# PE's order in a windowed attention: the products of probabilities by values of pair n-1 come ahead of the matmuls that add the maxima to the scores of pair n, not behind them

## The chip, the cores and the metric

The kernel runs on one core of a Trainium2 chip, in one launch. The metric is the device time of an execution in microseconds (us); lower is better.

## What is computed

The input x is 8 x 32 x 32 x 256 in float32. Two layers follow one another, each on a group-normalised copy of its input, each added back to it:

```python
x = x + _L0_conv_ref(_gn(x), qkv_w, qkv_b, bias_table)     # attention in windows of 8 x 8
x = x + _L1_conv_ref(_gn(x), W, b)                          # linear, then a spiking neuron over the 8 samples
# _L0_conv_ref, for each of 128 windows of 64 tokens and each of 16 heads of 16 channels:
attn = einsum('wihd,wjhd->whij', q * SCALE, k) + bias + MASK
attn = softmax(attn, axis=-1)
out  = einsum('whij,wjhd->wihd', attn, v)
```

_gn takes mean and variance of each sample in 32 groups of channels.

## The kernel before

x stays in SBUF for the whole run. The attention works on **strips**: a strip is one row of four windows (the code's `row`; 4 in a sample, 32 in all). A strip is worked off as two **pairs** of windows (n = 0 to 63). The code's k runs from 0 to 7 through the pairs of a sample; p = k % 2 is 0 for the first pair of a strip ("even pair") and 1 for the second ("odd pair"). The loop over samples 1 to 5 is a hardware loop, the others are written out.

Matmuls need more precision than one 16-bit or 32-bit reduced pass gives, so operands come as a high and a low part (xn_hi and xn_lo, k_hi and k_lo, v_hi and v_lo, p_hi and p_lo).

Every engine has its own program, in an order fixed by hand, and semaphores between them. In pair n:

- PE (TensorE): even pair: `project_q` and `project_k` of the next strip; odd pair: `project_v` of the next strip. Then `scores(n)`: bias and key-query products of the first half of the heads (L975, L977), the transpose of the maxima, `turn_maxima` (L992), the same products for the second half, and last the eight matmuls that add the negated maxima to the scores (L985). These eight wait until ScalarE has copied the transposed maxima (`max_rows`). They are called the **pick** matmuls here, after their weights, pick_max. Then `weigh_values(n-1)`: 24 matmuls of probabilities by values (L1008), here called **PV**, which in two pairs of a sample have a small matmul for the group statistics ahead of them (`beside`: L878 or L882). Then `max_scores(n+1)` (L952, L958), whose maxima will be needed by pair n+1, and `turn_attention(n-2)` (L1018).
- ACT (ScalarE): `normalise` or `xn_high` (even pair L461, odd pair L473, for the strip two ahead), `q_high` and `k_high` (L479, L492) or the first half of `v_high` (L501); `max_rows` (L570); in odd pairs the second half of `v_high`; then the four exponentials of pair n (L579, L580, two for each half of the heads), which wait for the pick matmuls; then `keep_attention(n-2)` (attn_cm, L543), which waits for `turn_attention`. In the trace's order of time, attn_cm and xn_hi or xn follow the exponentials.
- DVE (VectorE): low parts of q and k (L727, L739) or of v (L752); `attention_out(n-1)` (L769, L773), which waits for PV; the maxima of pair n+1 (neg_max, L759); statistics (L649).
- POOL (GpSimd): in odd pairs xn_lo (L386); p_lo of pair n (L424, after the exponentials); `add_attention(n-2)` (L413, after attn_cm); and once in a sample, in pair k = 2, 13 small instructions for the square roots of the next normalisation (L231 to L239). In the last sample they come at k = 4.
- SP: q and k of the next strip go to DRAM and come back stacked in another layout (k_spill, k_stack); `scores` of an even pair waits for them.

proj_ps holds q, k and v in turn: `project_q` waits until DVE has read the values (v_lo), and until xn_lo is there.

The first normalisation's set-up and the attention's first pairs share ACT, DVE and POOL with the building of bias tables (`bias_high`, `bias_variant`, `bias_low`). After the last pair come the LIF units (the spiking neuron), bound to each other in time order over the samples.

Of the kernel before, what the change touches and what calls it, by code (L numbers as in the profile page):

```python
# [5 lines left out]
def swin_attention_then_lif_kernel(nc, image, x, qkv_w, qkv_b, bias_table, lif_w, lif_b, out):  # L6
# [40 lines left out]
    with ctx:  # L47
# [134 lines left out]
        def wait(eng, s, value):  # L182

            if not isinstance(value, int) or value > 0:
                eng.wait_ge(s, value)
# [16 lines left out]
        def slot_total(row, y, per):  # L202

            return (row + (2 - y % 2)) * (per // 2)
# [5 lines left out]
        def is_first(n, lag):  # L210

            return isinstance(n, int) and n < lag

        def norm_beside(s, k):

            if has_sample(s, 1):
                return s + 1, (s + 1) * HALVES, HALVES, k - 1  # L220
            return SAMPLES, 0, EARLY, k - 3
# [19 lines left out]
        def is_last_pair(n):  # L241

            return isinstance(n, int) and n == PAIRS - 1

        def is_last_row(row, ahead=1):
            return isinstance(row, int) and row + ahead >= ROWS
# [626 lines left out]
        def _(pe):  # L873
            pe.wait_ge(const_step, 4)

            def average_means(norm, width, averages):
                pe.wait_ge(norm_dve, norm * NORM_STEPS + 1)
                pe.matmul(averages[:, 0:width], group_avg[:, :], moments[:, 0:width, 0], start=True, stop=True).then_inc(norm_pe, 1)  # L878

            def average_variances(norm, width, averages):  # L880
                pe.wait_ge(norm_dve, norm * NORM_STEPS + 4)
                pe.matmul(averages[:, NORMS:NORMS + width], group_avg[:, :], tiny[2][:, 0:width], start=True, stop=True)\  # L882
                  .then_inc(norm_pe, 1)
# [39 lines left out]
            def project_q(slot, r):  # L923
                pe.wait_ge(xn_lo_done, r + 1)
                wait(pe, v_lo_done, r)
                project_channels(banks[6], 0, xn_hi[slot], xn_lo[slot]).then_inc(q_ps_done, 1)

            def project_k(slot, r):
                wait(pe, attn_kept, 2 * r - 4)
                project_channels(banks[7], C, xn_hi[slot], xn_lo[slot], C).then_inc(k_ps_done, 1)  # L930

            def project_v(slot, r):
                pe.wait_ge(q_lo_done, r + 1)
                for p in range(2):
                    last = project_tokens(proj_ps[:, 0, p * C:(p + 1) * C], p, 2 * C, slot)
                last.then_inc(v_ps_done, 1)

            def variant(k, w):

                return 2 * (k // 2 == WROWS - 1) + (2 * (k % 2) + w == WCOLS - 1)  # L940
# [20 lines left out]
                                             start=False, stop=(h == 1 and mid == 1))  # L961
                last.then_inc(max_ps_done, 1)

            def scores(n, row, k):

                slot, p = k // 2 % 2, k % 2
                if p == 0:
                    pe.wait_ge(stacked[slot], slot_total(row, k // 2, 96))
                for h in range(HALVES):
                    wait(pe, p_hi_done, n * 2 + (h - 1))  # L970
                    for g in range(QUADS):
                        for w in range(2):
                            dst = score_ps[:, h, g * 128 + w * WS:g * 128 + (w + 1) * WS]
                            at = h * WCOLS + 2 * p + w
                            pe.matmul(dst, bias_k[:, variant(k, w), h * QUADS + g, :], both_parts[:, 0, :],  # L975
                                      start=(g == 0 and w == 0), stop=False)
                            pe.matmul(dst, k_stack[slot][:, g, at, :], q_stack[slot][:, g, at, :], start=False, stop=False)  # L977
                    if h == 0:
                        turn_maxima(n)
                pe.wait_ge(max_rows_done, n + 1)  # L980
                for h in range(HALVES):
                    for w in range(2):
                        for mid in range(2):
                            dst = score_ps[:, h, :].rearrange("p (m q w i) -> p m w q i", m=2, q=2, w=2)[:, mid, w, :, :]
                            last = pe.matmul(dst, pick_max[:, 4 * w + 2 * h + mid, :],  # L985
                                             max_rows[p][:, :].rearrange("p (q i) -> p q i", q=2),
                                             start=False, stop=(w == 1 and mid == 1))
                    last.then_inc(score_ps_done, 1)

            def turn_maxima(n):  # L990
                pe.wait_ge(neg_max_done, n + 1)
                pe.transpose(max_ps[:, 0, :].bitcast(f16)[0:16, 0:128], neg_max[:, :], ident_h[:, :])\  # L992
                  .then_inc(max_turned, 1)

            def weigh_values(m, row, k, beside=None):

                p = k % 2
                pe.wait_ge(p_lo_done, m * 2 + 2)
                if p == 0:
                    pe.wait_ge(v_lo_done, row + 1)  # L1000
                wait(pe, attn_done, m)
                if beside:
                    beside()
                for h in range(HALVES):
                    cols = pv_ps[:, h, 0:2 * WIN_N].rearrange("p (w g n) -> p w g n", w=2, g=QUADS)
                    for g in range(QUADS):
                        for at, (pp, vv) in enumerate(((p_hi, v_hi), (p_hi, v_lo), (p_lo, v_hi))):
                            last = pe.matmul(cols[:, :, g, :], pp[p][:, h * QUADS + g, :, :].rearrange("p w i -> p (w i)"),  # L1008
                                             vv[k][:, h, :, g, :, :].rearrange("p w e d -> p w (e d)"),
                                             start=(at == 0), stop=(at == 2))  # L1010
                last.then_inc(pv_ps_done, 1)

            def turn_attention(m, p):
                pe.wait_ge(attn_done, m + 1)
                wait(pe, attn_kept, m)
                tokens = attn[p][:, :, :, :].rearrange("p h n d -> p (h n d)")
                for h in range(HALVES):
                    last = pe.transpose(proj_ps[:, 1, h * 128:(h + 1) * 128], tokens[:, h * 128:(h + 1) * 128], ident[:, :])  # L1018
                last.then_inc(attn_turned, 1)
# [9 lines left out]
            def unit_products(m, t):  # L1029

                pe.wait_ge(unit_ready, m + 1)
                project_unit(banks[t], unit[t % 4]).then_inc(h_ps_done, 1)

            def pair(n, row, k, s):
                p = k % 2
                nxt = (k // 2 + 1) % 2
                if not is_last_row(row):
                    if p == 0:
                        project_q(nxt, row + 1)
                        project_k(nxt, row + 1)  # L1040
                    else:
                        project_v(nxt, row + 1)
                if is_first(n, 8):
                    pe.wait_ge(bias_lo_done, variant(k, 1) + 1)
                scores(n, row, k)
                norm, _, width, stage = norm_beside(s, k)
                beside = None
                if stage == 0:
                    beside = lambda: average_means(norm, width, spare_averages)
                if stage == 1:  # L1050
                    beside = lambda: average_variances(norm, width, spare_averages)
                if not is_first(n, 1):
                    weigh_values(n - 1, row if p else row - 1, (k - 1) % 4, beside)
                if not is_last_pair(n):
                    max_scores(n + 1, row + 1 if p else row, (k + 1) % BODY)
                if p == 0 and not is_last_row(row):
                    pe.wait_ge(k_lo_done, row + 2)
                if not is_first(n, 2):
                    turn_attention(n - 2, p)
                if is_last_pair(n):  # L1060
                    unit_products(0, 0)

            run(pe, pair)
            weigh_values(PAIRS - 1, ROWS - 1, 3)
            turn_attention(PAIRS - 2, 0)
# [50 lines left out]
```

## Time and profile before

| | |
|---|---|
| time of 3 runs | median 555.68 us (555.5 to 556.34) |
| the profiled execution | 557.95 us, its span 556.2 us |
| busy of the span: PE, weight loads | 475.5 us (85%), 425.9 us (77%) |
| busy: DVE, ACT, POOL | 445.3 us (80%), 415.5 us (75%), 272.0 us (49%) |
| granted TensorE clock, mean | 0.964 |

The attention takes most of the span: the first max_rows starts at 42.0 us and the last at 478.3 us. Before it is set-up, and after it are the LIF units. A timeline row of the trace gives the start in us, the duration, engine, line and operation; several equal instructions in a row are merged (xcount), and in square brackets stands how long the engine was idle before it and for what.

### The profile page before, as it was taken

Reading aid. Unit: us, or ns where it says so; the run is one execution under the profiler, and the core shown is the slowest. Engines: PE = TensorE matmul, PEld = TensorE weight load, DVE = VectorE, ACT = ScalarE, POOL = GpSimd, SP = SyncE. Lnnn points to the kernel's source line nnn. Section 1 sums busy time; section 2 is a strip of 40 time slices with the busy share of each in tenths; the row PEclk is TensorE's granted clock in tenths of the full one; section 3 lists DMA queues with packets and bytes.
Section 4 is the critical chain, followed back from the end, with each engine's and each line's share of the span. In section 5 each row is a group of like instructions: output and inputs, shape, how many; then the busy total and the mean of one; then the engine's idle time right before and its main releaser. Section 6 shows DMA issues by size and latency. Waiting matters only on the chain.

```text
span 556.2 us, 17802 instructions
## 1 busy us (share of the span) xinstructions
PE 475.5 (85%) x6504; PEld 425.9 (77%) x6504; DVE 445.3 (80%) x994; ACT 415.5 (75%) x1013; POOL 272.0 (49%) x379
## 2 busy tenths in 40 slices
PE   0364699898999899989998998999899977889997
PEld 0364688787888788888887887888788866778885
DVE  7856568868888889888987898788787877568897
ACT  2286578787889788888988998888889856745551
POOL 6134365556555656565566566655655546520000
PEclk9987789999999999999999999999999989879999
DMA  7176066766766677767776776656666545013333
GB/s 209 56 180 161 18 167 172 180 163 170 176 173 173 169 183 200 193 163 187 188 190 165 184 187 179 170 153 164 154 156 155 160 129 152 3 70 129 140 134 134
DMA packets 92576, 86.08 MB, mean 155 GB/s; under 512 B 41842, under 2 KB 63604, under 8 KB 92532
## 3 DMA queue, kind: packets, MB, share of 16 engines
q1 hardware_dynamic: 91808, 85.49, 58.0%
q8 instruction: 27, 0.44, 0.3%
q10 hardware_dynamic: 724, 0.01, 0.1%
q14 instruction: 17, 0.14, 0.1%
HBM read 47.72 MB, written 33.55 MB: 146 GB/s over the span
## 4 chain that ended last, share of the span: by engine, by line
PE 27%; issue 23%; POOL 22%; ACT 8%; DMA 8%; DVE 5%; SPq 3%; POOLq 1%; ACTq 1%; DVEq 0%
POOL p_lo L424 11%; POOL xc L413 5%; POOL xn_lo L386 4%; PE score_ps L895 3%; PE proj_ps L895 2%; PE pv_ps L895 2%; PE pv_ps L1008 2%; DMA k_stack<-k_spill1lo 2%; DMA k_spill1lo<-k_lo 2%; ACT v_hi L501 2%; PE proj_ps L908 2%; SPq L308 2%; PE max_ps L895 2%; PE score_ps L985 2%; PE proj_ps L910 2%
## 5 line engine op out<-in xcount | busy, mean ns | idle before, releaser
L424 POOL TENSOR_TENSOR p_lo<-probs,p_hi 128x512 f16<-128x512 f32 x128 | 146.6, 1166 | 165.0 <-ACT p_hi L580 165.0
L752 DVE TENSOR_TENSOR v_lo<-proj_ps,v_hi 64x128 f16<-64x128 f32 x256 | 74.1, 289 | 23.4 <-ACT v_hi L501 20.7
L579 ACT ACTIVATE probs<-score_ps 128x512 f32<-128x512 f32 x128 | 76.9, 601 | 19.5 <-PE score_ps L985 18.7
L975 PE MATMUL score_ps<-both_parts,bias_k 128*128 128x64 f16 x1024 | 83.1, 194 | 6.9 <-DMA k_stack<-k_spill1lo 4.0
L908 PE MATMUL proj_ps<-xn_hi,w_hi 128*128 128x256 f32 x256 | 76.7, 300 | 14.0 <-POOL xn_lo L386 13.4
L977 PE MATMUL score_ps<-q_stack,k_stack 96*128 96x64 f16 x1024 | 82.3, 194 | 0.0
L759 DVE TENSOR_REDUCE neg_max<-max_ps 128x16 f16<-128x1024 f32 x64 | 78.4, 1225 | 4.4 <-PE max_ps L958 2.4
L975 PEld LDWEIGHTS score_ps<-both_parts,bias_k 128*128 128x128 f16 x1024 | 67.7, 98 | 15.3 <-issue 4.6
L501 ACT ACTIVATE v_hi<-proj_ps 64x128 f16<-64x128 f32 x256 | 71.6, 280 | 10.1 <-PE proj_ps L920 7.1
L580 ACT ACTIVATE p_hi<-score_ps 128x512 f16<-128x512 f32 x128 | 77.3, 604 | 0.0
L909 PE MATMUL proj_ps<-xn_lo,w_hi 128*128 128x256 f32 x256 | 73.5, 287 | 0.0
L910 PE MATMUL proj_ps<-xn_hi,w_lo 128*128 128x256 f32 x256 | 73.3, 286 | 0.0
L977 PEld LDWEIGHTS score_ps<-q_stack,k_stack 96*128 96x128 f16 x1024 | 69.8, 98 | 0.0
L908 PEld LDWEIGHTS proj_ps<-xn_hi,w_hi 128*128 128x128 f32 x256 | 50.1, 196 | 19.3 <-issue 9.0
L739 DVE SCALAR_TENSOR_TENSOR k_lo<-proj_ps,parity_mask,k_hi 128x512 f16<-128x512 f32 x64 | 45.1, 746 | 21.6 <-ACT k_hi L492 21.6
L985 PE MATMUL score_ps<-max_rows,pick_max 128*128 128x128 f16 x512 | 41.2, 226 | 19.8 <-ACT max_rows L570 19.5
L1008 PE MATMUL pv_ps<-v_hi,p_hi 128*128 128x68 f16 x512 | 57.0, 198 | 0.5 <-POOL p_lo L424 0.5
L1008 PE MATMUL pv_ps<-v_lo,p_hi 128*128 128x68 f16 x512 | 57.1, 198 | 0.0
L1008 PE MATMUL pv_ps<-v_hi,p_lo 128*128 128x68 f16 x512 | 57.0, 198 | 0.0
L773 DVE TENSOR_TENSOR attn<-pv_ps,recip 64x256 f32<-64x256 f32 x128 | 54.1, 422 | 3.1
L952 PE MATMUL max_ps<-bias_q,ident_h 128*128 128x512 f16 x128 | 50.6, 396 | 4.4 <-ACT bias_q L510 4.4
L492 ACT ACTIVATE k_hi<-proj_ps,parity_mask 128x512 f16<-128x512 f32 x64 | 40.5, 684 | 17.7 <-PE proj_ps L910 17.7
(136 smaller groups left out, 1354.1 us busy)
## 6 DMA issues: line engine op xcount, KB each, us to landing
xc<-in_x_dram SPq DMA_DIRECT2D x32, 256.0 KB, 4.8
k_stack<-k_spill0hi SPq DMA_DIRECT2D x32, 256.0 KB, 4.2
k_stack<-k_spill1hi SPq DMA_DIRECT2D x32, 256.0 KB, 4.0
out_dram<-xc SPq DMA_DIRECT2D x32, 256.0 KB, 2.3
q_hi<-q_flat SPq DMA_DIRECT2D x128, 32.0 KB, 2.0
k_spill0hi<-k_hi SPq DMA_DIRECT2D x16, 256.0 KB, 2.2
k_spill0lo<-k_lo SPq DMA_DIRECT2D x16, 256.0 KB, 2.4
q_stack<-q_spill0hi SPq DMA_DIRECT2D x32, 128.0 KB, 2.7
```

Of the source, the lines that this page charges most:

```text
L424: pool.tensor_tensor(p_lo[p][:, quads, :, :].rearrange("p g w i -> p (g w i)"), probs[:, quads, :, :].rearrange("p g w i -> p (g w i)"), p ...
L501: last = act.activation(v_hi[2 * slot + p][e * WS:(e + 1) * WS, :, w, :, e, 0:D], v_part(p, w, e), ACT.Copy)
L579: act.activation(probs[:, quads, :, :].rearrange("p g w i -> p (g w i)"), score_ps[:, h, :], ACT.Exp)
L580: act.activation(p_hi[p][:, quads, :, :].rearrange("p g w i -> p (g w i)"), score_ps[:, h, :], ACT.Exp)\
L752: last = dve.tensor_tensor(v_lo[2 * slot + p][rows, :, w, :, e, 0:D], v_part(p, w, e), v_hi[2 * slot + p][rows, :, w, :, e, 0:D], ALU.subt ...
L759: dve.tensor_reduce(neg_max[:, :], max_ps[:, :, :].rearrange("p w (n j) -> p (w n) j", j=WS), AX.X, ALU.max, negate=True).then_inc(neg_max ...
L908: pe.matmul(dst, w_hi[:, c, cols], high[:, tok], start=(c == 0 and bias is None), stop=False)
L909: pe.matmul(dst, w_hi[:, c, cols], low[:, tok], start=False, stop=False)
L910: last = pe.matmul(dst, w_lo[:, c, cols], high[:, tok], start=False, stop=(c == HALVES - 1))
L975: pe.matmul(dst, bias_k[:, variant(k, w), h * QUADS + g, :], both_parts[:, 0, :], start=(g == 0 and w == 0), stop=False)
L977: pe.matmul(dst, k_stack[slot][:, g, at, :], q_stack[slot][:, g, at, :], start=False, stop=False)
L1008: last = pe.matmul(cols[:, :, g, :], pp[p][:, h * QUADS + g, :, :].rearrange("p w i -> p (w i)"), vv[k][:, h, :, g, :, :].rearrange("p w e ...
```

## The change

PV of pair n-1, with its small statistics matmul where it has one, is issued inside `scores(n)`, between the second half of the key-query products and the wait for max_rows. The pick matmuls come behind it. Nothing is added or removed. Only PE's order changes; the orders of ACT, DVE, POOL and SP are the same row for row.

```diff
-            def scores(n, row, k):
+            def scores(n, row, k, values_before):
...
                     if h == 0:
                         turn_maxima(n)
+                if not is_first(n, 1):
+                    weigh_values(n - 1, row if p else row - 1, (k - 1) % 4, values_before)
                 pe.wait_ge(max_rows_done, n + 1)
...
-                scores(n, row, k)
                 norm, _, width, stage = norm_beside(s, k)
                 beside = None
...
-                if not is_first(n, 1):
-                    weigh_values(n - 1, row if p else row - 1, (k - 1) % 4, beside)
+                scores(n, row, k, beside)
                 if not is_last_pair(n):
                     max_scores(n + 1, row + 1 if p else row, (k + 1) % BODY)
```

PE in pair 1, before: the last key-query products of the scores, the pick matmuls, the statistics matmul and the first PV matmuls.

```order
L975 MATMUL score_ps<-both_parts,bias_k 128x64
L977 MATMUL score_ps<-q_stack,k_stack 128x64
L985 MATMUL score_ps<-max_rows,pick_max 128x2x64 x8
L878 MATMUL pv_ps<-moments,group_avg 128x2
L1008 MATMUL pv_ps<-v_hi,p_hi 128x2x34
L1008 MATMUL pv_ps<-v_lo,p_hi 128x2x34
L1008 MATMUL pv_ps<-v_hi,p_lo 128x2x34
```

PE at the same place of the changed kernel (its lines behind L980 are two higher), first the front of PV:

```order
L975 MATMUL score_ps<-both_parts,bias_k 128x64
L977 MATMUL score_ps<-q_stack,k_stack 128x64
L878 MATMUL pv_ps<-moments,group_avg 128x2
L1010 MATMUL pv_ps<-v_hi,p_hi 128x2x34
L1010 MATMUL pv_ps<-v_lo,p_hi 128x2x34
L1010 MATMUL pv_ps<-v_hi,p_lo 128x2x34
```

and 21 PV matmuls later its end:

```order
L1010 MATMUL pv_ps<-v_hi,p_lo 128x2x34
L987 MATMUL score_ps<-max_rows,pick_max 128x2x64 x8
L952 MATMUL max_ps<-bias_q,ident_h 128x512
L958 MATMUL max_ps<-k_hi,q_hi 128x128 x4
L952 MATMUL max_ps<-bias_q,ident_h 128x512
```

The eight pick matmuls moved from ahead of PV to behind it; the matmuls of the maxima (L952, L958) now follow them directly.

PE in the last pair, n = 63, of the changed kernel: the end of PV of pair 62, the pick matmuls, the transpose of the attention and the first LIF unit.

```order
L1010 MATMUL pv_ps<-v_hi,p_lo 128x2x34
L987 MATMUL score_ps<-max_rows,pick_max 128x2x64 x8
L1020 MATMUL proj_ps<-ident,attn 128x128 x2
L893 MATMUL max_ps<-ones_r,b_rows 128x256
L895 MATMUL max_ps<-unit,w_lif 128x256 x2
L893 MATMUL max_ps<-ones_r,b_rows 128x256
```

Before, the same place reads:

```order
L1008 MATMUL pv_ps<-v_hi,p_lo 128x2x34
L1018 MATMUL proj_ps<-ident,attn 128x128 x2
L893 MATMUL max_ps<-ones_r,b_rows 128x256
L895 MATMUL max_ps<-unit,w_lif 128x256 x2
L893 MATMUL max_ps<-ones_r,b_rows 128x256
```

Here too all 24 PV matmuls of pair 62 now stand ahead of the last pick matmuls, on which the exponentials of pair 63 wait.

## Rows read from the trace of the kernel before

**Rows 1.** Windows: stretch, length, busy us of PE, PEld, DVE, ACT, POOL, PEclk, DMA share, GB/s

```profile
244.00:296.00 52.00, 48.63 (x769) 43.74 (x768) 44.82 (x104) 45.60 (x116) 30.93 (x41) 1.00 0.72 182
452.00:456.00 4.00, 3.92 (x42) 3.40 (x43) 1.76 (x6) 0.12 (x1) 0.32 (x1) 0.60 0.05 10
```

**Rows 2.** Waits of the whole span: total us, times, longest us

```profile
PE score_ps L985 <- ACT max_rows L570: 19.5, 45, 5.2
...
PE proj_ps L908 <- POOL xn_lo L386: 13.4, 8, 6.3
...
ACT v_hi L501 <- PE proj_ps L920: 7.1, 30, 0.7
```

**Rows 3.** Timeline of ACT in one strip

```profile
256.95 1.27 ACT L492 ACTIVATE k_hi<-proj_ps,parity_mask 128x512 f16<-128x512 f32 x2 [0.46 <-PE proj_ps L910]
...
258.84 0.60 ACT L579 ACTIVATE probs<-score_ps 128x512 f32<-128x512 f32 x1 [0.49 <-PE score_ps L985]
...
260.97 0.63 ACT L543 ACTIVATE attn_cm<-proj_ps,b_cols 128x128 f32<-128x128 f32 x2
261.49 0.63 ACT L473 ACTIVATE xn_hi<-xn 128x512 fp32r<-128x512 f32 x1
262.34 1.15 ACT L501 ACTIVATE v_hi<-proj_ps 64x128 f16<-64x128 f32 x4 [0.22 <-PE proj_ps L920]
...
263.80 1.16 ACT L501 ACTIVATE v_hi<-proj_ps 64x128 f16<-64x128 f32 x4
264.98 0.60 ACT L579 ACTIVATE probs<-score_ps 128x512 f32<-128x512 f32 x1
...
266.91 0.65 ACT L543 ACTIVATE attn_cm<-proj_ps,b_cols 128x128 f32<-128x128 f32 x2
```

**Rows 4.** Timeline of PE in the same strip

```profile
258.00 0.19 PE L977 MATMUL score_ps<-q_stack,k_stack 96*128 96x64 f16 x1
258.41 0.62 PE L985 MATMUL score_ps<-max_rows,pick_max 128*128 128x128 f16 x8 [0.22 <-ACT max_rows L570]
258.87 0.19 PE L1008 MATMUL pv_ps<-v_hi,p_hi 128*128 128x68 f16 x1
...
259.61 0.38 PE L952 MATMUL max_ps<-bias_q,ident_h 128*128 128x512 f16 x1
...
266.27 0.39 PE L908 MATMUL proj_ps<-xn_hi,w_hi 128*128 128x256 f32 x1
```

**Rows 5.** Timeline of DVE, the last v_lo of that strip

```profile
264.99 1.22 DVE L752 TENSOR_TENSOR v_lo<-proj_ps,v_hi 64x128 f16<-64x128 f32 x4 [0.30 <-ACT v_hi L501]
```

**Rows 6.** Timelines of PE and POOL in a strip with square roots

```profile
284.36 0.34 PE L882 MATMUL pv_ps<-tiny,group_avg 128*128 128x2 f32 x2
...
285.50 2.29 POOL L424 TENSOR_TENSOR p_lo<-probs,p_hi 128x512 f16<-128x512 f32 x2 [3.66 <-ACT p_hi L580]
...
293.40 0.38 PE L908 MATMUL proj_ps<-xn_hi,w_hi 128*128 128x256 f32 x1 [1.12 <-POOL xn_lo L386]
```

**Rows 7.** Timelines of DVE, ACT and POOL in pairs 1 and 2

```profile
56.74 0.16 DVE L678 TENSOR_SCALAR neg_mean<-pv_ps 128x2 f32<-128x2 f32 x1 [0.40 <-PE pv_ps L1008]
...
69.56 2.27 POOL L424 TENSOR_TENSOR p_lo<-probs,p_hi 128x512 f16<-128x512 f32 x2 [2.76 <-ACT p_hi L580]
...
72.49 0.63 ACT L543 ACTIVATE attn_cm<-proj_ps,b_cols 128x128 f32<-128x128 f32 x2 [2.12 <-PE proj_ps L1018]
...
73.19 0.74 POOL L413 TENSOR_TENSOR xc<-xc,attn_cm 128x256 f32<-128x256 f32 x1 [1.37 <-ACT attn_cm L543]
```

**Rows 8.** Waits of the first key-query product for k_stack, whole span

```profile
PE score_ps L975 <- DMA k_stack<-k_spill1lo: 4.0, 4, 2.5
...
PE score_ps L975 <- DMA k_stack<-k_spill0lo: 2.8, 3, 2.1
```

**Rows 9.** Timeline of PE, pair k = 3 of the last sample and the end

```profile
452.08 0.58 PE L878 MATMUL pv_ps<-moments,group_avg 128*128 128x14 f32 x2 [3.79 <-DVE moments L671]
...
482.66 0.20 PE L1008 MATMUL pv_ps<-v_hi,p_hi 128*128 128x68 f16 x1 [0.49 <-POOL p_lo L424]
```

## The prediction

> **What bounds the kernel now.** I read the busy shares by windows first. In a whole sample of the steady part PE is busy 48.6 of 52 us, ACT 45.6, DVE 44.8, POOL 30.9, with PE's clock at its upper level [rows 1]. Three engines stand near 90% and none is full, so what binds must be a loop through several engines. The waits come next [rows 2]. PE waited for max_rows in front of the pick matmuls 45 times, which is the gap that the change fills. But ACT waited for PE 30 times in front of v_hi: nearly every strip, always in the same place. And PE waited for xn_lo of POOL 8 times: once in the set-up, once in the start, and once in each of six later samples.
>
> The timeline of one strip shows the loop [rows 3 to 5]. k_hi starts at 256.95. The pick matmuls start at 258.41, the exponentials of the even pair 0.43 us later at 258.84. v_hi starts at 262.34, because PE had finished project_v only then. From there it is ACT and DVE alone: v_hi second half at 263.80, v_lo from 264.99 to 266.21, and project_q of the next strip on PE at 266.27, 0.06 us behind v_lo. So from the start of v_hi to project_q is 3.93 us, and PE has idle time before project_q. What moves the start of v_hi moves the strip; PE's gap in the odd pair costs nothing.
>
> **The steady strips.** Look at the even pair on PE [rows 4]. The last key-query product is issued at 258.00, the pick matmuls at 258.41, PV from 258.87 to 259.61, that is 0.74 us. Moved ahead, PV starts at 258.03 and the pick matmuls at 258.77, 0.36 us later than before. Two paths lead from there to v_hi.
>
> By PE: pick to v_hi took 3.93 us (258.41 to 262.34), now without PV 3.19, which gives 261.96.
>
> By ACT: exponentials 0.43 us behind pick, at 259.20. In the odd pair ACT works without a wait from the exponentials to attn_cm, 264.98 to 266.91, 1.93 us; that gives 261.13. attn_cm to xn_hi is 0.52 us (260.97 to 261.49), and xn_hi, as long as attn_cm (0.63 us), should be followed as fast: 262.17 [rows 3].
>
> The later one counts: 262.17 instead of 262.34. The gap on PE gives back 0.38 us, but the exponentials start 0.36 later, and ACT takes over the bound. A plain strip gains 0.17 us. Bounds: 0.05 if v_hi waits for the full end of xn_hi, 0.38 if ACT did not bind. The odd pair's PV now needs p_lo of the even pair. p_lo starts when about half of the exponentials' 1.93 us is over, some 1.1 us with the step to POOL, and lasts 2.29 us [rows 6]: it ends at about 259.20 + 1.1 + 2.3 = 262.6. PV is wanted when the odd pair's products are issued. In the even pair those end 1.05 us behind the projection (256.95, when k_hi follows it, to 258.00), so here at 261.96 + 1.05 = 263.0 [rows 3, 4]. It just fits.
>
> Of the 31 steps from strip to strip three belong to the start, seven (below) wait for transfers or pass nothing on because the next one does, two lie at the end, and six have roots. 13 are left: 13 x 0.17 = -2.2 us.
>
> **The strips with square roots.** In pair k = 2 POOL works through p_lo, the residual, 13 root instructions and xn_lo in one row; project_q waits for its end. From p_lo's start at 285.50 to project_q at 293.40 are 7.90 us, PE having waited 1.12 us there, and p_lo had waited for the exponentials [rows 6]. So here the loop goes pick, exponentials, POOL, project_q, and a later pick is paid in full. The pick matmuls are later by 0.36 us and by the statistics matmul L882, which moves with PV: between 0.03 us (the issue pace in the rows 4) and its 0.34 [rows 6], I take 0.19. That is +0.55 us, six times [rows 2]: +3.3 us.
>
> **The start.** Here the change helps. In pairs 1 and 2 ACT is held up by the bias tables, and the longest wait for max_rows is 5.2 us [rows 2]; PV fits into it whole. After it attn_cm waits 2.12 us for PE's transpose, and the residual on POOL waits 1.37 us for attn_cm [rows 7]; the roots and xn_lo follow it. Without PV (0.74 us, about double at the lower clock level that PE shows behind long idle time, as the 0.60 in the rows 1) in front of the transpose, the residual can start where p_lo ends, 69.56 + 2.27 = 71.83 instead of 73.19: 1.36 us. DVE's wait of 0.40 us for PV in pair 1 [rows 7] falls away too and moves the bias tables forward. Together -1.75 us. It would be -1.1 if PE's clock stayed up.
>
> **Strips that wait for k_stack.** Seven times the scores waited for the transfer, 6.8 us in all [rows 8]. The first is pair 0, which has no PV; the 2.5 us one belongs to the last strip, and the 2.1 us one, the only other long wait, I count at nothing (at most 0.2). In the other four max_rows is there when the key-query products end, so the pick matmuls are later by the whole 0.74 us. PE's path from the exponentials to v_hi is 3.93 - 0.43 = 3.50 us, ACT's 1.93 + 0.52 + 0.52 = 2.97, so 0.53 is slack and 0.21 is lost. The transfers hang on the k_hi of the strip before, so a gain there is not passed on either. Two of the four follow each other, and there the next wait swallows one loss: +0.6 us.
>
> **Pair k = 3 of the last sample.** Its L878 waits 3.79 us for DVE's moments [rows 9]. The pick matmuls stood ahead of this wait and now stand behind it. They take 0.46 us (258.41 to 258.87 [rows 4]), up to double after the idle time, where the clock was at 0.60 on average [rows 1]. max_scores, the transpose and the projections come later by that: +0.85 us. The exponentials behind them move by over 4 us, into time in which ACT was busy 0.12 of 4 us [rows 1].
>
> **The end.** In pair 63 nothing but PV stands between the key-query products and pick, and max_rows is there. PV of pair 63 waits for p_lo, the last of that chain [rows 9]. So the LIF units start later by PV: +0.75 us.
>
> **Sum.** -1.75 - 2.2 + 3.3 + 0.6 + 0.85 + 0.75 = +1.55 us. The steps were read in the profiled execution, which took 557.95 us against a median of 555.68, 0.4% more; the difference is put on the median: **557.2 us**, 0.3% slower. Nothing is added to any engine's work; PE's gaps come back and the wait moves to ACT and POOL.
>
> **Rivals.**
>
> (a) *ACT does not take over in the plain strips.* Then v_hi starts at 261.96, each plain strip gains 0.38 instead of 0.17, 2.7 us more: 554.4 us, faster. It decides from a gain of 0.34 us per strip on. For it: ACT idles 0.46, 0.49 and 0.22 us in the strip [rows 3]. Against it: the first two come ahead of the exponentials again, and the path of ACT adds up to 0.21 us more than that of PE. The same time comes out if a root strip costs only 0.1, should the roots' start not follow p_lo.
>
> (b) *PE is the bound and every gap comes back.* The gap is 258.00 to 258.41, less one issue step, 0.38 us in the even pair; with as much in the odd one it is 0.76 per strip, 24 us over 32 strips: 533 us. Against it stands project_q directly behind v_lo, and behind xn_lo in the root strips. The Trainium skill gives this rule in "Perfetto Trace Analysis", section "Optimization Strategies": keep the matmul engine as highly utilised as possible. By that rule the time would be about 533 us. The same page goes on that the engines that block it are to be improved, and with this the trace agrees: they are ACT and POOL here.
>
> (c) *No difference that can be told.* Start gain and losses meet: a root strip costs 0.4, pair k = 3 only 0.46, which takes 1.3 us off: 555.9 us.
>
> (d) *PV waits for p_lo in the odd pair.* The margin is 0.3 us. A PV late by more than about 1 us in all would push the odd pair's exponentials; if every plain strip then lost 0.1 instead of gaining 0.17, the time is 560.7 us. Against: p_lo begins as soon as p_hi ends.
>
> **How the numbers follow.** A measurement of this kernel tells about 0.2% from no change, 1.1 us. Chances: my forecast, 556.8 to 558.8 us, 0.44; (d) and other losses above that 0.08; (c) 0.26; (a) 0.19; (b) 0.03. So slower 0.52, same 0.26, faster 0.22. The range has to take in (c) and most of (a): bounds of the terms are -1.1 to -1.9 for the start, -0.7 to -4.9 for the plain strips, +2.3 to +4.2 for the root strips, +0.45 to +0.9 for pair k = 3. Not all fall on one side: 554.0 to 559.3 us.
>
> **What the new profile would show.** The wait of PE for max_rows in even pairs gone. ACT's idle time before the exponentials near 0.85 us in place of 0.49, and its 0.22 before v_hi gone, in nearly all 30 places. Plain strips (k_hi to k_hi) 0.17 us shorter, strips with roots 0.55 longer, still ended by POOL's xn_lo. The first wait of PE at pick still 5 us long, but the residual of pair 0 on POOL about 1.75 us earlier. PE at the last sample's L878 still waiting, with pick behind. I am wrong if v_hi still waits for PE in plain strips, if root strips are no longer, or if PE waits for p_lo in odd pairs.

## The result, and the profile after

The changed kernel takes 565.46 us (562.2 to 566.18, 4 runs) beside 556.01 us for the kernel before in the same runs; the ratio is 1.0149, 95% interval 1.0099 to 1.02. That is 8.3 us slower by the ratio, 9.5 us by the medians, where 1.5 us was forecast. The profiled execution took 566.18 us with a span of 564.5 us, 8.3 us more than the span before.

The page of the changed kernel: busy time of the engines, and the granted clock of PE in 40 slices.

```profile
PE 474.3 (84%) x6504; PEld 430.0 (76%) x6504; DVE 441.2 (78%) x994; ACT 407.3 (72%) x1013; POOL 272.2 (48%) x379
...
PEclk9987799998999899989998999899999979889999
```

Every engine has as many instructions as before. The waits of the whole span (total us, times, longest):

```profile
ACT probs L579 <- PE score_ps L987: 40.8, 37, 5.8
...
PE proj_ps L908 <- POOL xn_lo L386: 23.2, 8, 6.3
...
PE proj_ps L908 <- DVE v_lo L752: 11.2, 18, 0.8
...
PE score_ps L987 <- ACT max_rows L570: 7.4, 2, 4.0
PE score_ps L975 <- DMA k_stack<-k_spill1lo: 7.1, 4, 4.3
...
ACT v_hi L501 <- PE proj_ps L920: 1.7, 2, 1.3
```

Read beside [rows 2], they say that the change did to PE what it does on paper: the waits for max_rows fell from 45 to 2, and those of v_hi for PE from 30 to 2. In their place ACT's wait in front of the exponentials grew from 18.7 us (33 times) to 40.8 us (37 times), PE waits for v_lo in plain strips, and PE's wait for POOL's xn_lo grew from 13.4 to 23.2 us in the same 8 places.

A plain strip on ACT, as in [rows 3]:

```profile
315.23 1.26 ACT L492 ACTIVATE k_hi<-proj_ps,parity_mask 128x512 f16<-128x512 f32 x2 [0.48 <-PE proj_ps L910]
...
317.48 0.60 ACT L579 ACTIVATE probs<-score_ps 128x512 f32<-128x512 f32 x1 [0.85 <-PE score_ps L987]
...
319.41 0.65 ACT L543 ACTIVATE attn_cm<-proj_ps,b_cols 128x128 f32<-128x128 f32 x2
319.90 0.67 ACT L473 ACTIVATE xn_hi<-xn 128x512 fp32r<-128x512 f32 x1
320.43 1.15 ACT L501 ACTIVATE v_hi<-proj_ps 64x128 f16<-64x128 f32 x4
```

The exponentials start 2.25 us behind k_hi instead of 1.89, and v_hi 5.20 us behind it instead of 5.39: 0.19 us gained, with ACT working through without a gap. The next k_hi starts at 327.76, 12.53 us later, beside 12.72 for the same strip of the same sample before (309.58 to 322.30).

The 8 us are in the strips with square roots. The start of project_q on PE in one, to compare with [rows 6], and then the windows of the same stretches:

```profile
297.74 0.39 PE L908 MATMUL proj_ps<-xn_hi,w_hi 128*128 128x256 f32 x1 [2.74 <-POOL xn_lo L386]
```

```profile
294.90:297.70 2.80, 0.10 (x1) 0.00 (x0) 2.66 (x7) 2.80 (x7) 2.21 (x7) 1.00 1.05 226
297.70:302.60 4.90, 4.86 (x31) 4.82 (x32) 1.99 (x5) 0.97 (x3) 2.93 (x3) 0.65 0.12 41
```

PE stood idle for 2.74 us where it had stood 1.12. In the projections that follow, its granted clock is 0.65 on average, most of it the lower level (1.2 GHz), and they take 4.86 us, where the same work took 3.4 us at 1.00 before:

```profile
293.40:296.80 3.40, 3.40 (x32) 3.35 (x33) 2.68 (x6) 1.88 (x5) 2.90 (x3) 1.00 0.23 60
```

So a root strip takes 16.4 us and not the 14.9 of the forecast. The Trainium skill describes the clock that way in "TensorE: Matmul & The Clock Gate", section "What's actually happening": the throttled level is the default, and activity releases it. The trace agrees in five of the six root strips, as in this one, 1.00 before the idle time and 0.65 behind it; in the sixth, in sample 6, PE idled 2.68 us and its clock stayed at 1.00.

Where the 8.3 us are, from the starts of k_hi in both traces. One k_hi lies in the set-up, at 29.4 us before and 30.0 after; "first" is the one of pair 0, and each later strip has one:

```
stretch                                   before    after   difference
set-up to the first k_hi                   40.87    41.62     +0.75
first k_hi to that of k = 4, sample 0      41.19    39.29     -1.90
next three strips                          41.68    39.62     -2.06
strip with roots, sample 1                 14.37    18.22     +3.85
strips with roots, samples 2 to 5       4 x 14.36  4 x 16.41  +8.19
strip with roots, sample 6                 14.30    14.90     +0.60
all other strips, up to four from the end 192.25   190.22     -2.03
next four strips, to the last k_hi         56.82    59.28     +2.46
last k_hi to p_lo of pair 63               21.41    22.65     +1.24
p_lo of pair 63 to the end                 75.87    73.07     -2.80
```

The third and fourth row belong together. Before, PE waits 2.10 us for k_stack in one strip of the third row, the granted clock of the 4.5 us behind that wait is 0.62, and the strip takes 16.21 us. After, PE waits 1.59 us in front of the same first key-query product in one strip of the third row (14.34 us; the trace puts this wait down to issue) and 1.64 us for k_stack in the root strip, and its clock stays at 1.00 behind both. Together the two rows are +1.8.

Two rows can't be put down to the change. No PV comes ahead of the first k_hi, and it starts at 40.87 to 43.43 us in the 13 traces, so the +0.75 lies within what executions differ by. The last row is PE's clock again: the LIF units start at a granted clock of 0.69 in the 10 us from 490 before, and at 1.00 in the 10 us from 501 after. Why is not shown, but the order in the last pair does not decide it: with the old order this stretch took 72.7 us in e10_start_only and e11_old_at_end, 74.3 in e6_best and e8_before_late_pool, and 75.9 before.

### The profile page after: what moved, and what is told of

Same layout as the page of the kernel before. It is cut to its first block, busy times and chain, and to the rows that moved or that the text cites. A ratio compares the mean times of both kernels' runs of the same rounds, so it can differ in the third digit from the quotient of the medians.

```text
span 564.5 us, 17802 instructions
## 1 busy us (share of the span) xinstructions
PE 474.3 (84%) x6504; PEld 430.0 (76%) x6504; DVE 441.2 (78%) x994; ACT 407.3 (72%) x1013; POOL 272.2 (48%) x379
## 4 chain that ended last, share of the span: by engine, by line
PE 30%; issue 18%; ACT 16%; POOL 15%; DVE 9%; DMA 6%; SPq 4%; POOLq 1%; ACTq 0%; DVEq 0%
POOL p_lo L424 7%; ACT v_hi L501 5%; ACT p_hi L580 4%; PE proj_ps L908 3%; POOL xn_lo L386 3%; POOL xc L413 3%; PE pv_ps L1010 3%; PE proj_ps L909 3%; PE proj_ps L910 3%; DMA k_stack<-k_spill1lo 3%; PE proj_ps L895 2%; PE score_ps L895 2%; PE pv_ps L895 2%; PE max_ps L895 2%; PE score_ps L975 2%
## 5 line engine op out<-in xcount | busy, mean ns | idle before, releaser
L908 PE MATMUL proj_ps<-xn_hi,w_hi 128*128 128x256 f32 x256 | 80.1, 313 | 34.4 <-POOL xn_lo L386 23.2
L579 ACT ACTIVATE probs<-score_ps 128x512 f32<-128x512 f32 x128 | 77.0, 602 | 41.5 <-PE score_ps L987 40.8
L752 DVE TENSOR_TENSOR v_lo<-proj_ps,v_hi 64x128 f16<-64x128 f32 x256 | 74.2, 290 | 32.5 <-ACT v_hi L501 29.4
L908 PEld LDWEIGHTS proj_ps<-xn_hi,w_hi 128*128 128x128 f32 x256 | 53.4, 208 | 40.5 <-POOL xn_lo L386 18.6
L909 PE MATMUL proj_ps<-xn_lo,w_hi 128*128 128x256 f32 x256 | 76.8, 300 | 0.0
L910 PE MATMUL proj_ps<-xn_hi,w_lo 128*128 128x256 f32 x256 | 76.5, 299 | 0.0
L1010 PE MATMUL pv_ps<-v_hi,p_hi 128*128 128x68 f16 x512 | 55.7, 196 | 1.3 <-POOL p_lo L424 1.3
L1010 PE MATMUL pv_ps<-v_hi,p_lo 128*128 128x68 f16 x512 | 55.8, 196 | 0.0
L1010 PE MATMUL pv_ps<-v_lo,p_hi 128*128 128x68 f16 x512 | 55.6, 195 | 0.0
L952 PE MATMUL max_ps<-bias_q,ident_h 128*128 128x512 f16 x128 | 50.8, 396 | 4.4 <-ACT bias_q L510 4.4
L958 PEld LDWEIGHTS max_ps<-k_hi,q_hi 128*128 128x128 f16 x512 | 41.2, 101 | 16.5 <-issue 2.5
```

The source lines that it names most:

```text
L579: act.activation(probs[:, quads, :, :].rearrange("p g w i -> p (g w i)"), score_ps[:, h, :], ACT.Exp)
L752: last = dve.tensor_tensor(v_lo[2 * slot + p][rows, :, w, :, e, 0:D], v_part(p, w, e), v_hi[2 * slot + p][rows, :, w, :, e, 0:D], ALU.subt ...
L908: pe.matmul(dst, w_hi[:, c, cols], high[:, tok], start=(c == 0 and bias is None), stop=False)
L909: pe.matmul(dst, w_hi[:, c, cols], low[:, tok], start=False, stop=False)
L910: last = pe.matmul(dst, w_lo[:, c, cols], high[:, tok], start=False, stop=(c == HALVES - 1))
```

## The experiments

Two theories were set against each other. **Theory 1**: the longer idle time of PE before project_q lowers its clock, and that costs 1.5 us in a root strip on top of the 0.55 us that the later pick costs. **Theory 2**: the later pick alone, through POOL, costs the 2.05 us.

**1. The idle time filled with 16 small matmuls** (e1_fill), on top of the change. keep_clock waits for v_lo, then issues 16 matmuls of 128x256 into the bank that project_q overwrites; its body is left out here.

```diff
+                        if k == 4 and has_sample(s, 1):
+                            keep_clock(row, 16)
                         project_q(nxt, row + 1)
```

> The changed kernel, and in pair k = 4 of samples 0 to 6, between the wait for v_lo and project_q, 16 matmuls on PE whose result project_q overwrites; they fill some 1.9 us in which PE had nothing to do. Theory 1 (PE idles 2.8 us before project_q in strips with roots, its clock falls to the half level, and the projections take 4.86 instead of 3.4 us): strips with roots fall from 16.4 to 14.9 us, five of them, 7 to 7.5 us less in all, some 558 us. Theory 2 (the later pick alone costs the 2.05 us, through POOL): strips with roots stay at 16.4 us and the time at 565 us.

Measured: 588.02 us, ratio 1.0567 (1.052 to 1.0615). 588 us is far from both expectations. The root strips did shorten, to 14.94 to 14.96 us in three samples, 15.57 and 15.90 in two, and 17.85 in sample 1, all six with the projections at a clock of 1.00, as theory 1 expects. But the strip from k = 6 to k = 0 grew from 12.5 to between 18.2 and 20.7 us in samples 2 to 5. PE's timeline at such a place:

```profile
227.08 0.58 PE L908 MATMUL proj_ps<-xn_hi,w_hi 128*128 128x256 f32 x1 [5.12 <-issue]
```

PE waits for nothing that the profile shows. This is the turn of the hardware loop over the samples. The time as a whole therefore decides nothing, and the run opened a question of its own, which experiments 5 and 11 take up.

**2. The old order in pairs k = 2 alone** (e2_old_at_roots). `scores` takes one argument more and issues PV inside only where it is true; that part is left out here.

```diff
+                values_early = k != 2 or is_first(n, 8)
+                scores(n, row, k, beside, values_early)
+                if not values_early and not is_first(n, 1):
+                    weigh_values(n - 1, row if p else row - 1, (k - 1) % 4, beside)
```

> The changed kernel with PV behind the pick matmuls, as before, in pair k = 2 of samples 1 to 7 alone. Both theories: strips with roots back at 14.4 us, from 16.4. Theory 1: p_lo and xn_lo are 0.55 us earlier, and PE's idle time before project_q is 0.55 us shorter, about 2.2 us; if the clock still falls there, the strips are 15.8 us instead and the time 562; if not, 554 us, below the kernel before. Theory 2: 14.4 us and 554 us whatever the clock does.

Measured: 556.05 us, ratio 0.9986 (0.9956 to 1.0015). Root strips 14.33 to 14.35 us in samples 2 to 5, clock 1.00. The idle time is 1.11 us, as in the kernel before, and not the 2.2 us that was expected. One edit in one pair of eight takes the whole loss away; it does not tell the theories apart.

**3 and 4. The change in odd pairs, and in even pairs, alone** (e3_odd_only, e4_even_only; values_early is p == 1, and p == 0).

> PV ahead of the pick matmuls in odd pairs alone. v_lo binds project_q in plain strips and the even pair's exponentials are where they were, so plain strips stay at 12.75 us. In strips with roots POOL is not later, but PE reaches project_q some 0.4 us sooner and idles 1.6 us. Theory 1: the clock holds at that length, 14.4 us; at the start 0.4 us gained, at the last sample's k = 3 0.9 and at the end 0.75 lost, some 557 us. Theory 2: the same. If idle time of 1.6 us is enough to lower the clock, 564 us.

> PV ahead of the pick matmuls in even pairs alone. Plain strips 12.57 us. In strips with roots the pick matmuls are 0.56 us later and so is xn_lo, but PV of the odd pair still fills 0.74 us of PE's idle time, which is about 2.1 us. Theory 1: the clock holds, strips with roots 14.9 us, some 556.5 us; or it falls at 2.1 us too, 16.4 us and 564 us. Theory 2 (the later pick alone): 16.4 us, 564 us, with PE's clock at its upper level in the projections.

Measured: odd 557.97 us, ratio 1.0015 (0.9983 to 1.0046), root strips 14.35 to 14.36 us in samples 1 to 5, plain strips as before (12.72 to 12.80). PE idled 1.12 us in the root strips, not the 1.6 expected: in pair k = 3 of such a strip the pick matmuls had no wait to fill. Even 565.35 us, ratio 1.0122 (1.0065 to 1.018), plain strips 12.53 to 12.60, root strips 16.41 to 16.44 in samples 2 to 5. The loss and the gain of the steady part both belong to the even pair. PE's gap in the odd pair is worth nothing in plain strips, as the prediction said: with it filled, PE idles 0.15 to 0.49 us for v_lo in front of project_q, where the kernel before shows at most 0.06. In the even-only kernel the idle time and the clock behind it are

```profile
297.80 0.38 PE L908 MATMUL proj_ps<-xn_hi,w_hi 128*128 128x256 f32 x1 [2.14 <-POOL xn_lo L386]
```

```profile
297.80:302.30 4.50, 4.50 (x25) 4.50 (x26) 1.94 (x5) 0.94 (x3) 2.88 (x3) 0.62 0.13 41
```

so the clock falls after 2.14 us as after 2.74, in samples 1 to 5, and theory 2 had expected it at its upper level. In sample 6 of the same execution PE idled 1.99 us and the clock stayed at 1.00: 14.84 us for the strip.

**5. The idle time filled with 2 float32 matmuls** (e7_after_2), on top of the change: the same keep_clock with 2 matmuls of 128x512.

> The changed kernel, PE's idle time before project_q of pair k = 4 filled with 2 float32 matmuls of 512 columns (some 1.7 us, overwritten by project_q) instead of 16 small ones. Theory 1 (the clock): root strips 14.9 us in all samples, projections in 3.4 us, and, the loop on PE being only 2 matmuls longer, no stall at the loop's start: some 558 us. Theory 2 (the later pick alone): 16.4 us, 565 us. If the 5 us stall in the strip k = 6 to k = 0 of the kernel with 16 matmuls comes back, it is not the number of added instructions.

Measured: 559.93 us, ratio 1.0063 (1.0033 to 1.0093), that is 5.5 us less than the changed kernel by the medians, 4.8 by the ratios and 7.5 between the two profiled spans. The timeline of PE in a root strip, then the windows:

```profile
291.23 1.98 PE L1040 MATMUL proj_ps<-w_lif,ident 128*128 128x512 f32 x4 [0.60 <-DVE v_lo L752]
293.40 0.39 PE L908 MATMUL proj_ps<-xn_hi,w_hi 128*128 128x256 f32 x1 [0.19 <-POOL xn_lo L386]
```

```profile
293.40:296.80 3.40, 3.40 (x32) 3.36 (x33) 1.69 (x5) 0.93 (x3) 2.89 (x3) 1.00 0.10 28
```

The order is that of the changed kernel, the pick is as late, PE does more work, and the projections are back at 3.40 us: the root strips of samples 1 to 5 are all 14.90 to 14.92 us (in sample 6 it is 16.09, with PE waiting 1.08 us for k_stack in it). Both parts of theory 1 have their size here: 14.35 + 0.55 = 14.90 for the lateness, and 16.4 - 14.9 = 1.5 for the clock. Theory 2 falls.

**6. The kernel before, with POOL made late** (e8_before_late_pool): PE's order untouched.

```diff
                     norm_roots(pool, root_pool, (norm - 1) * ROOT_STEPS, norm, first, width)
+                    if not is_first(n, 8) and has_sample(s, 1):
+                        pool.memset(w_raw[:, :, 0:832], 0.0)
```

> The kernel before, with a memset of 128 x 1664 elements on POOL (some 1.5 us) behind the roots of pair k = 2 in samples 1 to 6, on a buffer that nobody reads any more. xn_lo is 1.5 us later and PE's idle time before project_q 2.7 us instead of 1.25. Theory 1 (idle time lowers the clock, whatever the order): root strips 14.36 + 1.5 + 1.5 = 17.4 us in most samples, some 572 us. Theory 2 (PE's order is what matters): 15.9 us, 565 us, projections in 3.4 us.

Measured: 569.38 us, ratio 1.0213 (1.0167 to 1.0258). PE idled 2.52 to 2.54 us in five root strips and 2.32 in the sixth. In three the clock fell and in three it did not; two that lie 55 us apart:

```profile
303.88:308.38 4.50, 4.50 (x26) 4.49 (x26) 1.21 (x4) 0.84 (x2) 2.87 (x3) 0.66 0.00 0
359.25:363.75 4.50, 4.50 (x59) 4.33 (x59) 1.58 (x4) 1.95 (x4) 2.89 (x3) 1.00 0.10 31
```

The strips are 17.09 and 15.75 us, 1.3 us apart, with the same work and the same wait. So the fall needs no change of order, and an idle time of this length brings it often, not always. What else decides is not shown. The forecast of 572 us took it for nearly certain.

**7. Two Newton steps instead of three** (e9_two_newton), on top of the change.

> The changed kernel with two Newton steps instead of three for the square roots (the third is left out). POOL's chain in pair k = 2 is 4 instructions, 1.1 us, shorter. Theory 1: PE idles 1.7 us instead of 2.8 before project_q, the clock holds, root strips 16.4 - 1.1 - 1.5 = 13.8 us, some 551 us. Theory 2: the strips are 1.1 us shorter, 15.3 us, some 558 us. If the clock falls at 1.7 us too, 15.3 us as well, but with a clock below 1 in the projections.

Measured: 553.39 us, ratio 0.993 (0.9901 to 0.9958). Root strips 13.81 to 13.82 us in four samples (14.28 in sample 2, 13.75 in sample 6), the 13.8 that theory 1 had worked out.

```profile
290.16 0.39 PE L908 MATMUL proj_ps<-xn_hi,w_hi 128*128 128x256 f32 x1 [1.68 <-POOL xn_lo L386]
```

```profile
290.16:294.66 4.50, 4.50 (x60) 4.34 (x61) 3.01 (x6) 3.13 (x7) 2.89 (x3) 1.00 0.39 97
```

Four small instructions less on POOL, 1.1 us, took 12 us off the time of the changed kernel: 1.1 + 1.5 us in a root strip where the clock had fallen.

**8. The change only where it paid** (e6_best): values_early is false in pair k = 2 of samples 1 to 7, in k = 3 and 4 of the last sample and in the last pair.

> PV ahead of the pick matmuls only where that paid or cost nothing in the profile: not in pair k = 2 of samples 1 to 7, not in pairs k = 3 and 4 of the last sample, not in the last pair. Against the kernel with the old order in k = 2 alone (plain strips 12.57 us, root strips 14.35 us, 556.05 us) the last sample's k = 3 gives back some 0.9 us and the last pair 0.75. Theory 1 and theory 2 both expect some 554 us, a ratio to the kernel before of 0.995 to 0.998.

Measured: 554.61 us, ratio 0.9948 (0.9924 to 0.9973), 0.5% faster than the kernel before and 2% faster than the changed one.

**9. The start alone** (e10_start_only): values_early is n < 3.

> PV ahead of the pick matmuls in pairs 1 and 2 alone, everything else as before. The start term of the prediction by itself: 1.75 us forecast, 1.9 us read in the changed kernel's profile (k_hi to k_hi). If it stands alone, strips as before (12.75 and 14.36 us) and 554.7 us, a ratio of 0.997. Rival: the gain at the start is lost again in the next waits for k_stack, since the transfers keep their own time; then 556.5 us, ratio 1.000.

Measured: 554.2 us, ratio 0.9958 (0.9926 to 0.9991). From the first k_hi to that of k = 4 in sample 0 it takes 39.39 us, 1.80 less than before. It is as fast as e6_best; the two intervals overlap. In e6_best the plain strips are shorter by 0.17 us, but from the k_hi of k = 4 in sample 0 to the last one it is 376.26 us beside 376.96 here, 0.7 us and not the 2.8 that its 16 or so shorter strips add up to. The place of the difference is one strip of sample 1. In e6_best PE waits 1.85 us for k_stack in it, the granted clock of the 4.5 us behind that wait is 0.62, and the strip takes 15.84 us; in e10_start_only it waits 1.60 us in the same strip, its clock stays at 1.00, and the strip takes 14.16 us. Up to the end of this strip e6_best loses 1.2 us against e10_start_only, and from there to the last k_hi it gains 1.9. Whether the fall comes with the order or by the execution, one trace of each cannot say.

**10. The old order at the end** (e11_old_at_end): not in pair k = 3 of the last sample and not in the last pair.

> The changed kernel with the old order in pair k = 3 of the last sample and in the last pair alone. By the prediction's terms that returns 0.85 and 0.75 us, the stretch from the moments' end to k_hi back from 8.4 us to 7.0 us, and some 563.9 us against 565.5 for the changed kernel; root strips stay at 16.4 us. Rival: after the long wait PE's clock is low either way, and the end waits for the transfers of the last strip, so that nothing comes back: 565.5 us.

Measured: 564.51 us, ratio 1.0122 (1.0068 to 1.0175), beside 1.0149 for the changed kernel; the intervals overlap, so the time does not decide. From the end of the 14 moments on DVE to k_hi it is 7.56 us, beside 8.38 in the changed kernel and 6.98 before. But e10_start_only, with the old order there too, takes 8.26 us. The windows behind the wait in e11_old_at_end, and then in e10_start_only:

```profile
461.30:465.30 4.00, 3.88 (x39) 3.36 (x40) 1.65 (x6) 0.00 (x0) 0.36 (x1) 0.50 0.12 27
```

```profile
449.80:453.80 4.00, 3.81 (x39) 3.29 (x39) 1.62 (x7) 0.00 (x0) 0.42 (x1) 0.50 0.40 81
453.80:458.10 4.30, 4.30 (x35) 4.26 (x33) 2.69 (x5) 1.47 (x5) 0.73 (x1) 0.75 0.00 0
```

0.50 for 4 us where it was 0.60 before [rows 1]. How long the lower level lasts behind such a wait moves this stretch by as much as the term that was to be measured. It stays open.

**11. Sixteen small matmuls in the kernel before** (e5_before_16).

> The kernel before with the 16 small matmuls ahead of project_q in pair k = 4. PE does not need them here: its clock is at the upper level in these projections anyway, and from v_lo to xn_lo it has 1.1 us where the 16 take 2.2, so a root strip is some 1 us longer, +7 us in seven samples. Theory A (the loop's body on PE, 16 matmuls and their weight loads longer, does not stay loaded and its instructions are fetched anew in each turn): also a stall put down to issue of 4 to 5 us at the loop's start in samples 2 to 5, and more packets on the instruction queue than 27; 585 us. Theory B (the stall came from the changed order): no stall, 27 packets, 563 us.

Measured: 592.47 us, ratio 1.0616 (1.0562 to 1.0671), with 4 stalls put down to issue, of up to 6.5 us. The instruction queue of this kernel:

```profile
q8 instruction: 63, 1.03, 0.8%
```

It was 27 packets and 0.44 MB before, and is 27 in the changed kernel and in the one with 2 float32 matmuls; e1_fill has 63 too. The root strips are 15.12 us in most samples, 0.8 us longer, and the strip with the loop's turn 20.4 to 21.3 us instead of 12.7. So theory A holds and B falls: the stall came with the 16 matmuls and not with the changed order. That it is the number of instructions, and not something else in them, rests on these two kernels and e7_after_2.

## Why the prediction was wrong

*What bounds the kernel, and the plain strips.* Right in the main. The bound went from PE's project_v to ACT's path from the exponentials, v_hi starts 5.20 us behind k_hi (forecast 5.22), and the strips are 0.17 to 0.2 us shorter. One reading under it was not: the row at 266.27 [rows 4] has no idle time, so "PE has idle time before project_q" does not stand in it; PE comes there just in time. The conclusion held all the same, and e3_odd_only shows it: the gap in odd pairs is worth nothing in the steady part. PV waited for p_lo of the even pair nowhere in the steady part, so rival (d) did not come in. Rival (a) did not either: ACT did take over.

*The start.* Right, -1.75 forecast, -1.90 measured, -1.80 alone, and by the step named: the residual on POOL starts directly behind p_lo, with no wait for attn_cm, and attn_cm waits 0.41 us for the transpose instead of 2.12 [rows 7].

*The strips with roots.* **This is the term that failed**, +3.3 us for six strips. "A later pick is paid in full", +0.55 us: e7_after_2 measures exactly that, 14.90 against 14.35. But the term stopped there. The same change stretches PE's idle time before project_q from 1.12 to 2.74 us. The prediction listed the 1.12 us wait in its rows, used it to show that POOL binds, and never asked how long the wait would be afterwards. The timelines of PE in pair k = 3 show where it comes from, first the kernel before (k_hi at 282.44), then the changed one (k_hi at 286.24):

```profile
289.15 0.22 PE L992 MATMUL max_ps<-ident_h,neg_max 128*16 128x128 f16 x1 [0.64 <-DVE neg_max L759]
...
291.89 0.39 PE L1018 MATMUL proj_ps<-ident,attn 128*128 128x128 f32 x2
```

```profile
291.87 0.22 PE L994 MATMUL max_ps<-ident_h,neg_max 128*16 128x128 f16 x1
...
294.61 0.39 PE L1020 MATMUL proj_ps<-ident,attn 128*128 128x128 f32 x2
```

Counted from k_hi, project_q starts 0.54 us later (11.50 instead of 10.96), and PE is through with its last work before it 1.08 us earlier (8.37 instead of 9.45). Of this 0.37 us are the filled wait for max_rows in pair k = 2, and 0.71 us come with the wait for DVE's neg_max in pair k = 3, which is gone. In e4_even_only a new wait of 0.45 us for max_rows in pair k = 3 takes part of it back, which leaves 2.14 us. Behind 2.7 us the clock fell in five of six samples, at 1.5 us each: 7.5 us, more than the 6.8 us by which the measured 8.3 us exceed the forecast 1.5. The prediction even used the lower level for the start and for the last sample, from [rows 1], and not here.

*Waits for k_stack.* About as forecast in sum: outside the root strips the steady strips gained 2.0 us where 13 x 0.17 = 2.2, less up to 0.6, had been worked out. Where the waits fall moves from kernel to kernel by 1 to 2 us per strip.

*Pair k = 3 of the last sample, and the end.* Not settled in size. The stretch behind the moments grew by 1.4 us where 0.85 was forecast, but part of this is clock. From the last k_hi to p_lo of pair 63 it is +1.24 us instead of +0.75. The 2.8 us that the LIF units then gave back were in no term.

*Rival (b)*, every gap of PE comes back, is dead: 43 of 45 waits for max_rows are gone and the time rose. Its price was also taken wrong: 24 us off the median of 555.68 are 531 us, not 533.

## What to carry to other kernels

When an engine is moved ahead of a wait, work out not only what the wait is filled with but where the engine will stand idle instead, and how long. For TensorE that place has a price beyond its length: the matmuls behind it may run at half the clock, and if they are on the loop that binds, this can cost more than the order wins: 1.5 us in a root strip here, against 0.2 us won in a plain one. A move that pays in some repetitions and costs in one kind is worth making a condition: here the two pairs at the start carried all of the gain that could be measured.

## What the runs showed of the hardware

Behind idle times of PE of 2.0 to 2.8 us in front of the same projections, the granted clock of the next 4.5 us was 0.62 to 0.66 in 18 of 24 cases (changed kernel 5 of 6, e4_even_only 5 of 6, e11_old_at_end 5 of 6, e8_before_late_pool 3 of 6) and 1.00 in the others. Behind idle times of 0.9 to 1.7 us at this place it was 1.00 in all 36 strips of samples 1 to 6 in six kernels (before, e2, e3, e6, e9, e10). Within the first group, the length does not tell which case comes: 2.52 us went both ways.

These lengths are no limits for other places. In front of the first key-query product of a strip, behind 90 us, the 13 traces hold 16 waits of PE of 1.5 to 2.4 us. Behind six of them the clock fell, the shortest 1.50 us (e8_before_late_pool, 0.64 in the next 4.5 us), and behind ten it did not, the longest 2.36 us (e3_odd_only). The kernel before has one of the six. Behind the 21 idle times of 3.8 us and more (in front of the last sample's L878 in all 13 traces, and at the loop's turns in two) it was at most 0.66 each time.

A loop body longer by 16 matmuls and their weight loads brought a stall of 4.2 to 6.5 us at each turn of the hardware loop, a strip there that is 5.6 to 8.6 us longer, and 36 more packets on the instruction queue; 2 matmuls of 512 columns, which fill the same time, cost nothing there. The Trainium skill, "Runtime: NRT & Kernel Launch", section "Instruction fetch mechanics", says that a taken branch whose target is not held forces a fetch before execution can go on. The trace agrees, with 63 packets instead of 27; no run here shows how long a body may be.
